# Moving the experts' first bias from TensorE's accumulation to ScalarE and VectorE in a fused two-layer kernel

## The reference

```python
for e in range(E):                       # E = 16, D = I = 128
    we = jnp.sum(weights * (indices == e), axis=-1)
    h = jax.nn.silu(x2 @ W1[e].T + b1[e]) * (x2 @ W3[e].T + b3[e])
    y = y + (h @ W2[e].T + b2[e]) * we[:, None]
```

## Time and profile before

| | |
|---|---|
| runs | 2837.02, 2846.48 and 2848.29 us; median 2846.48 |
| profiled execution, its own time | 2834.54 us |
| its span from first to last instruction | 2832.5 us |
| TensorE busy | 2383.8 us, 84% |
| VectorE busy | 1938.1 us, 68% |
| GpSimd busy | 1734.4 us, 61% |
| ScalarE busy | 1632.5 us, 58% |
| mean granted TensorE clock | 0.94 of full speed |

### The profile page before, as it was taken

One profiled execution on the slowest core, in us unless ns is written; L12 is line 12 of the kernel. 1 busy time (PEld: TensorE's weight loads), 2 busy tenths in 40 slices (PEclk: granted clock), 3 DMA queues, 4 the chain that ended last, 5 costly groups with the idle time before them and its releaser, 6 DMA issues.

```text
span 2832.5 us, 37071 instructions
## 1 busy us (share of the span) xinstructions
PE 2383.8 (84%) x9792; PEld 1218.1 (43%) x9792; DVE 1938.1 (68%) x3181; ACT 1632.5 (58%) x4156; POOL 1734.4 (61%) x2247
## 2 busy tenths in 40 slices
PE   5889988999898998989899898989899998868332
PEld 3555544444444444444444444444444444322110
DVE  2444568676767768676777768686776867675766
ACT  3655566666566666666566666656666665533432
POOL 1012268585857768585867858585866857576534
PEclk9999999999999999999999999999999999979665
DMA  6424365655555665665545565656556565334432
GB/s 136 47 47 72 59 137 115 139 101 113 111 115 113 105 139 105 133 107 118 115 99 122 109 142 93 127 109 130 111 104 114 115 138 97 91 94 114 114 94 63
DMA packets 497979, 304.95 MB, mean 108 GB/s; under 512 B 349817, under 2 KB 416297, under 8 KB 497321
## 3 DMA queue, kind: packets, MB, share of 16 engines
q1 hardware_dynamic: 497772, 302.59, 53.0%
HBM read 242.21 MB, written 26.74 MB: 95 GB/s over the span
## 4 chain that ended last, share of the span: by engine, by line
PE 44%; DVE 24%; issue 14%; ACT 10%; POOL 5%; DMA 1%; SPq 0%; ACTq 0%; DVEq 0%; POOLq 0%
PE bank L515 9%; PE bank L842 7%; DVE work L1116 7%; PE bank L800 5%; DVE zh L835 3%; PE bank L542 3%; PE bank L1146 2%; PE bank L960 2%; ACT th L828 2%; PE bank L617 2%; DVE step L934 2%; DVE nmax L522 2%; PE bank L860 2%; ACT probs L532 2%; PE bank L572 2%
## 5 line engine op out<-in xcount | busy, mean ns | idle before, releaser
L1110 POOL TENSOR_TENSOR work<-work,bc 128x512 f32<-128x512 f32 x512 | 653.2, 1284 | 130.1 <-PE bank L1146 103.9
L1116 DVE TENSOR_TENSOR_SCAN work<-bank,work 128x512 f32<-128x512 f32 x512 | 621.3, 1214 | 123.8 <-POOL work L1110 68.6
L855 POOL TENSOR_TENSOR zh<-zh,w_bc 128x512 f32<-128x512 f32 x256 | 324.9, 1269 | 542.2 <-DVE zh L848 542.1
L1123 POOL TENSOR_TENSOR work<-work,bc 128x512 f32<-128x512 f32 x448 | 577.7, 1295 | 120.0 <-DVE work L1116 120.0
L532 ACT ACTIVATE probs<-bank,nmax 128x256 f32<-128x256 f32 x1024 | 475.0, 471 | 212.7 <-DVE nmax L522 210.6
L515 PE MATMUL bank<-ke,q_all 96*128 96x256 f32 x2048 | 553.1, 393 | 12.2 <-DMA q_all<-q_rows 12.2
L1099 ACT ACTIVATE bank<-work,neg_a 128x510 f32<-128x510 f32 x512 | 352.6, 689 | 345.8 <-DVE work L1116 336.6
L515 PEld LDWEIGHTS bank<-ke,q_all 96*128 96x128 f32 x2048 | 380.8, 196 | 217.4 <-issue 154.7
L522 DVE TENSOR_REDUCE nmax<-bank 128x2 f32<-128x512 f32 x512 | 347.6, 679 | 163.4 <-PE bank L515 154.0
L842 PE MATMUL bank<-h_b,w_t 128*128 128x512 f32 x512 | 292.1, 653 | 113.0 <-DVE zh L835 105.3
L542 PEld LDWEIGHTS bank<-ident,probs 128*128 128x128 f32 x2048 | 256.1, 145 | 260.1 <-issue 175.2
(11 more groups left out here) (193 smaller groups left out, 2535.5 us busy)
## 6 DMA issues: line engine op xcount, KB each, us to landing
work<-dt_rows SPq DMA_DIRECT2D x256, 512.0 KB, 4.9
w_bc<-w_rows_d SPq DMA_DIRECT2D x256, 256.0 KB, 4.8
ke<-ke SPq DMA_DIRECT2D x128, 256.0 KB, 5.1
bc<-bc_rows SPq DMA_DIRECT2D x64, 256.0 KB, 6.2
x_in<-in_x SPq DMA_DIRECT2D x32, 256.0 KB, 5.0
q_all<-q_rows SPq DMA_DIRECT2D x512, 8.0 KB
dt_rows<-step SPq DMA_DIRECT2D x16, 512.0 KB, 2.8
dt_rows<-step SPq DMA_DIRECT2D x32, 256.0 KB, 2.4
```

Of the source, the lines that this page charges most:

```text
L855: nc.gpsimd.tensor_tensor(zh[:, n % 3, :], zh[:, n % 3, :], w_bc[:, n % WB, :], ALU.mult).then_inc(m_p, 1)
L1110: nc.gpsimd.tensor_tensor(hb[at % HB], ring[n % RING][:, 1, :], bc[:, s, :], ALU.mult).then_inc(s_dbx, 1)
L1116: nc.vector.tensor_tensor_scan(hb[at % HB], decay_bank(p, m)[:, :], hb[at % HB], 0.0, ALU.mult, ALU.add).then_inc(s_h, 1)
L1123: nc.gpsimd.tensor_tensor(hb[at % HB], hb[at % HB], bc[:, SG + batch(m)[2], :], ALU.mult).then_inc(s_hc, 1)
```

## The change

The bias b1 is no longer added in PSUM. Line 799 goes away, with the split parts of b1, the row of ones and the ten steps at the start. Two columns hold b1 and b1/2 with a value for each partition. ScalarE computes th = tanh(bank/2 + b1/2). Because VectorE's instruction has room for one column operand, and needs it for b1 now, the "+ 1" goes to ScalarE as a second instruction on `th`, which waits for the first; VectorE computes (bank + b1) * th. Many numbers of `AT` are new.

```diff
-            nc.tensor.matmul(gate_bank(p)[:, :], b1_p[:, e * P:(e + 1) * P], ones, start=True, stop=False)
-            nc.tensor.matmul(gate_bank(p)[:, :], w1_t[:, e, :], h_b[:, p % 2, :], start=False, stop=True).then_inc(m_g, 1)
+            nc.tensor.matmul(gate_bank(p)[:, :], w1_t[:, e, :], h_b[:, p % 2, :], start=True, stop=True).then_inc(m_g, 1)
...
-            nc.scalar.activation(th[:, :], gate_bank(p)[:, :], ACT.Tanh, scale=0.5).then_inc(m_t, 1)
+            nc.scalar.activation(th[:, :], gate_bank(p)[:, :], ACT.Tanh, scale=0.5, bias=b1_h[:, e:e + 1]).then_inc(m_th, 1)
+            act.wait_ge(m_th, n + 1)
+            nc.scalar.activation(th[:, :], th[:, :], ACT.Copy, bias=1.0).then_inc(m_t, 1)
...
-            nc.vector.scalar_tensor_tensor(zh[:, n % 3, :], th[:, :], 1.0, gate_bank(p)[:, :], ALU.add, ALU.mult).then_inc(m_a, 1)
+            nc.vector.scalar_tensor_tensor(zh[:, n % 3, :], gate_bank(p)[:, :], b1_c[:, e:e + 1], th[:, :], ALU.add, ALU.mult).then_inc(m_a, 1)
...
-            f_mix_tensor=527, s_decay_scalar=0, m_tanh_scalar=2, a_turn_scalar=8, a_exp_scalar=3, a_values_scalar=42,
+            f_mix_tensor=526, s_decay_scalar=0, m_tanh_scalar=2, a_turn_scalar=8, a_exp_scalar=3, a_values_scalar=41,
```

More of the change, by code:

```diff
@@ L86, in build @@
         w2_t = sb("w2_t", [P, NE, P])
+        b1_c = sb("b1_c", [P, NE])
+        b1_h = sb("b1_h", [P, NE])
         b3_c = sb("b3_c", [P, NE])
@@ L233, in build @@
         m_in = [sem(f"m_in{k}") for k in range(WB)]
-        m_g, m_t, m_a, m_u, m_b, m_p, m_w2 = (sem("m_" + n) for n in ("g", "t", "a", "u", "b", "p", "w2"))
+        m_g, m_th, m_t, m_a, m_u, m_b, m_p, m_w2 = (sem("m_" + n) for n in ("g", "th", "t", "a", "u", "b", "p", "w2"))
         b_y, b_back, b_x = sem("b_y"), sem("b_back"), sem("b_x")
@@ new lines, in build @@
+            a_out_tensor=[79, 144], a_out_scalar=[81, 145], s_end_vector=[450, 502],
+            a_spread_sync=[[-28, -28, -12, 4], [20, 36, 52, 68]], a_scatter_sync=[[-22, 4], [37, 69]], x_a_sync=-110,
+            x_res_sync=91, a_store_sync=-34, m_store_sync=182, m_fetch_sync=-6, s_rows_sync=377,
+            s_rows_in_sync=[377, 379, 383, 385], s_store_sync=[369, 373], s_fetch_sync=-14, f_store_sync=534,
+            a_scores_tensor=0, m_gate_tensor=1, m_up_tensor=3, m_down_tensor=10, a_turn_tensor=5, a_values_tensor=38,
@@ new lines, in build @@
+            a_norm_scalar=-52, a_turned_scalar=-46, a_keys_scalar=-40, a_values_in_scalar=-37, a_query_scalar=-35,
+            b_norm_scalar=159, b_turned_scalar=160, m_logits_scalar=166, m_weights_scalar=182, m_end_scalar=326,
+            s_norm_scalar=340, s_turned_scalar=342, s_conv_scalar=[351, 359], s_step_scalar=[366, 367], s_rows_scalar=374,
+            s_z_scalar=[391, 399], f_out_scalar=509, f_turned_scalar=526, f_norm_scalar=523, f_mix_scalar=527, s_scan_vector=1,
+            a_max_vector=1, m_up_vector=4, m_silu_vector=2, a_inverse_vector=33, a_scale_vector=42, a_stats_vector=-90,
@@ L292, in build @@
+            f_root_gpsimd=517, s_step_vector=[367, 370],
         )
@@ L1614, in setup_vector @@
             nc.vector.tensor_scalar(conv_w[:, :, :], conv_w[:, :, :], 0.5, None, ALU.mult)
+            nc.vector.tensor_scalar(b1_h[:, :], b1_c[:, :], 0.5, None, ALU.mult)
             nc.vector.tensor_scalar(b2_r, b2_r, 2.0, None, ALU.mult).then_inc(b2_done, 1)
@@ L1617, in setup_vector @@
             nc.vector.tensor_scalar(neg_a[:, :], neg_a[:, :], -1.0, None, ALU.mult).then_inc(s_setv, 1)
-        B1_AT = [24 + 8 * k for k in range(10)]
         SETUP, LATE = AT["a_query_tensor"] + 2, AT["m_logits_tensor"] - 1
@@ L1776 @@
         "wo_x": wo_x, "e_shift": e_shift, "wg_t": f["L0_ffn_Wg"].T, "w1_t": cols(f["L0_ffn_W1"]),
-        "w3_t": cols(f["L0_ffn_W3"]), "w2_t": cols(f["L0_ffn_W2"]), "b1_r": f["L0_ffn_b1"], "b3_c": f["L0_ffn_b3"].T,
-        "b2_r": b2, "one_of": np.eye(BPARTS, dtype=one),
-        "c_t": np.concatenate([f["L0_c"].T, f["L1_c"].T], 1), "wmod": np.concatenate([f["L0_wmod"], f["L1_wmod"]], 1),
+        "w3_t": cols(f["L0_ffn_W3"]), "w2_t": cols(f["L0_ffn_W2"]), "b1_c": f["L0_ffn_b1"].T, "b3_c": f["L0_ffn_b3"].T,
+        "b2_r": b2, "c_t": np.concatenate([f["L0_c"].T, f["L1_c"].T], 1), "wmod": np.concatenate([f["L0_wmod"], f["L1_wmod"]], 1),
         "win_t": f["L1_attn_W_in"].T, "conv_w": halves(f["L1_attn_conv_w"][:, 0, :]), "conv_b": halves(f["L1_attn_conv_b"][:, None]),
```

76 lines of the change are left out of this document (12 added, 64 removed).

## The result

The changed kernel takes 2859.3 us (median of 6 runs, 2857.7 to 2862.1) against 2844.7 for the kernel before on the same chip (6 runs). The ratio of the runs is 1.0055, 95% interval 1.0039 to 1.0070: 0.55% slower, where 1.5% was forecast. The profiled execution lies at 2862.1, its span is 2860.1.

A forecast was written before the change was run, and what follows sets the result against it. Bound: TensorE's work plus its in-order queue's waits, chiefly the gate-tanh-silu-up chain. 15 x (3.6 - 0.7) - 4.6 + 3 = +42 on the profiled 2834.5, plus 12 for the median: 2888 us; own range 2862 to 2915, overall 2828 to 2932.

The forecast's parts named there:

- rival 2: A draw: new waits and removed work cancel, within 14 us of 2846; chance 0.15.
- What is added to the chain: Gate to up matmul: tanh's bias column +0.10, the addition 0.66, silu's column operand +0.07 us; silu 0.83 later if uncovered.
- Who pays it: Sixteen experts of a pair, sorted by what their steps wait for: +3.6 us a pair at unchanged positions.
- ScalarE's load: ScalarE rises from 100.2 to 115 us a pair, no new bound; the chunk's exponential behind the addition is covered.
- partly covered: Three experts where other TensorE or VectorE work hides part of the longer chain: 0.93 us a pair together.
- What the new positions do: Changed places of instructions in the table: -0.7 us a pair, bounds -2.5 and +1.7.
- inverse and spreading ahead of the silu: On VectorE, four times a pair: +0.15 us at one place; with bank 3's copy ahead of a tanh, +0.28.
- The table loads: Two more on ScalarE a pair, 1.28 us each, one covered: tanh about 0.85 us later, bounds 0.4 and 1.3.
- At the norm: In front of the experts, TensorE's 1.9 us wait for ScalarE: -0.35 us a pair, including small moves.
- The start: Splitting b1 in the first pair goes away: 4.6 us saved once.
- rival 1: Positions win it back, also through fewer lower-clock stretches: faster, 2811 us if up-matmul waits grow only 3; chance 0.20.
- Rival 3: Much slower: ScalarE's queue late for the exponentials too, or more lower-clock stretches, 45 us on top, 2933; chance 0.15.

The follow-up runs named there:

- d_nobias: The kernel before without its bias matmul, everything else as it is: 2777.4 us, ratio 0.9787.
- f_dg_behind: The changed kernel with one position undone, inverse and spreading behind the silu again: 2875.2 us, ratio 1.0128.
- e_splus: The changed kernel with the softplus positions undone, so 34 table loads instead of 62: 2854.5 us, ratio 1.0058.
- a_oldpos: The changed kernel with the tables AT and FIRST of the kernel before: 2903.5 us, ratio 1.0237.

## Why the prediction was right or wrong

The direction was right and the size was not: 2888 us against 2859.3, a change of 0.55% where 1.5% was forecast. The 28.7 between them are two parts. The ledger said +42 from profile to profile, and it was +27.6; and 12 us were added for the median, where the changed kernel's median lies 2.8 under its profiled execution. The time is inside the range of 2828 to 2932, but 2.7 us under the forecast's own range and at the upper edge of rival 2, the draw.

- **What is added to the chain**: right. 0.09, 0.63 + 0.03 and 0.07 stand for 0.10, 0.66 and 0.07.
- **Who pays it** (+3.6 a pair; with start and end some +52 for the arithmetic): too low. At the old positions it was +66, and +88 without the blocked products. The step that failed is in "ScalarE's load": "What stands behind the addition in its queue is the exponential of the chunk". The copy of bank 3 stands there too, and TensorE asks for it at once: 2.7 us a pair (5.4 in two) where there was 0.05. I had followed what waits for the silu, and not everything that ScalarE's queue holds. Nor had I counted that part of the removed matmul's gain is lost at the copy `probs_t`: 2.4 us a pair for 0.8, and 2.1 in d_nobias. That a steady pair at the old positions still came near, 165.6 us against 161.1 (+4.5 for +3.6), is luck: ahead of the up matmul the wait grew by 5.7 us (26.6 against 15.3 in two pairs) and not by 8.6, and these 2.9 us too many stood against the 4.3 that were missed. Of the five kinds of expert, the three "partly covered" ones have no row.
- **What the new positions do** (-0.7 a pair, -10 in all): the step that failed most. They give the new arithmetic 44 us in all, where the sum had 10, of which 2.1 in each steady pair. The term "inverse and spreading ahead of the silu ... the copy of bank 3 ahead of a tanh adds about as much: +0.28 together" had the wrong sign in both halves: the copy ahead of the tanh takes 2.25 us a pair from TensorE's wait for it, and the spreading's place ahead of the silu is worth 16 us (f_dg_behind). The first half is read from traces, the second was run. The bound of -2.5 a pair was nearly reached.
- The table loads: 0.85 a pair counted, 13 us; e_splus puts them between nothing and 5. The drain of 1380 ns that the prediction quotes doesn't show: in the changed kernel 61 of the 62 loads start within 0.02 us of the end of what stood ahead of them, 46 are followed within 0.02 us, and the other 16 are followed by an instruction that waits for a matmul or a transfer. The earlier trace rows had it right.
- At the norm (-0.35): the wait for y_a is 2.2 us after and 1.9 before, and a new one of 1.8 for y_x (another of the norms) stands at the same matmul's line. So there is no gain at the norm, but about +2 a pair, which other waits give back.
- Against the 2837 us beside them, the arithmetic was 14 us dearer than counted (66 for 52) and the positions gave 34 more (44 for 10). So a steady pair came out nearly right, +2.4 for +2.9, by errors that cancel; the fifteen pairs together grew by 34.7 us for 43.5.
- The start gave 1.7 us from profile to profile (first gate at 174.4 instead of 176.1), but one profile can't tell: in the eleven profiled kernels without the split the first gate comes at 167.1 to 175.2 us, mean 170.5, in the nine with it at 172.4 to 182.6, mean 177.8. The 4.6 were not too much. From the last pair's first gate to the end it is 290.2 us after and 295.6 before, -5.4 where +3 was predicted. At the old positions it is 300.2, so the arithmetic did cost about what was counted there, and the new positions take 10 us off.
- **The frame**: "the runs shown have their median 12 us above it, so I put the changed kernel's median at 2888". This step fails by 14 us. The kernel before varies from run to run, and its pairs take 158.1 us without a stretch of lower clock and 161.3 to 162.0 with 10.2 us of it. The changed kernel's steady pairs are nearly all alike, and its profiled execution is at the top of its runs. A profiled execution's distance from its median belongs to that kernel and doesn't carry over.
- **Checks of the profile**: TensorE's 141 us a pair were 139.9 (the removed matmuls took 6.1 us of busy time with them, 5.0 were counted), the period of 163 was 163.6, ScalarE's 115 were 114.6, the loads 62. The wait ahead of the up matmul was 12.3 and not 14 or more.
- **The rivals**: the positions did win something back, as rival 1 said, but by ScalarE's copy and not by the clock. Low clock is 8.8 us a steady pair in the changed kernel and was 8.2 before. Rival 3's late queue of ScalarE is what a_oldpos shows, though at the copies and not at the exponentials; the new positions remove the larger part of it.

Open: how the 46 us divide over the single positions; why the short chain falls into the blocked rhythm and the long one doesn't, beyond that it meets GpSimd's run at another moment; whether the clock explains the two prices of the bias matmul; and what the skip product's edit gives alone.

## What to carry to other kernels

An arithmetic edit and a table of positions can't be priced apart, nor added: run the square of both (old and new of each) before believing either. When an instruction is put into an in-order queue, list everything behind it that another engine asks for at once, not only the next link of its own chain. And when leaving out work gives less than it should, look for an instruction whose own length has grown: here one product after the other that took six times its time hid some 60 of the addition's 78 us.
